# Attention scores in units of three PSUM banks, and diagonal blocks cut at 64, in a layer-norm, attention and expert kernel

## Time and profile before

| what | value |
|---|---|
| median of three runs | 719.63 us (718.04 to 719.94) |
| profiled execution: span from first to last instruction | 717.2 us |
| around the span, by the median | 2.4 us |
| PE busy (matmuls) | 657.9 us, 92% |
| DVE busy | 533.2 us, 74% |
| ACT busy | 497.1 us, 69% |
| POOL busy | 452.1 us, 63% |
| mean granted PE clock | 0.968 |

### The profile page before, as it was taken

One profiled execution on the slowest core, in us unless ns is written; L12 is line 12 of the kernel. 1 busy time (PEld: TensorE's weight loads), 2 busy tenths in 40 slices (PEclk: granted clock), 3 DMA queues, 4 the chain that ended last, 5 costly groups with the idle time before them and its releaser, 6 DMA issues. The chain is left out here.

```text
span 717.2 us, 18299 instructions
## 1 busy us (share of the span) xinstructions
PE 657.9 (92%) x5817; PEld 401.3 (56%) x5817; DVE 533.2 (74%) x1344; ACT 497.1 (69%) x817; POOL 452.1 (63%) x548
## 2 busy tenths in 40 slices
PE   3877468999999999999999999999989999999987
PEld 2765212333333336899999999999943333333323
DVE  7799987888888886554544446666656999999956
ACT  3999357999998996344444444444468899988983
POOL 6465428688888887775600036777636877677782
PEclk9999759999999999999999999999989999999987
DMA  6996595444454447955332234454424544446331
GB/s 172 285 274 216 157 246 102 97 104 86 103 114 103 113 88 186 214 143 144 109 87 73 73 91 120 112 124 114 121 50 80 115 84 109 110 115 128 76 96 37
DMA packets 185863, 89.21 MB, mean 124 GB/s; under 512 B 114608, under 2 KB 175312, under 8 KB 185680
## 3 DMA queue, kind: packets, MB, share of 16 engines
q1 hardware_dynamic: 177472, 70.70, 41.0%
q0 software_dynamic: 8336, 17.84, 9.4%
HBM read 30.17 MB, written 32.24 MB: 87 GB/s over the span
## 5 line engine op out<-in xcount | busy, mean ns | idle before, releaser
L775 ACT ACTIVATE prob<-psum 128x1024 f32<-128x1024 f32 x320 | 314.6, 1026 | 55.3 <-PE psum L867 45.7
L785 ACT ACTIVATE prob<-psum,prob 128x256 f32<-128x256 f32 x284 | 117.3, 470 | 132.3 <-PE psum L997 129.4
L892 PE MATMUL psum<-prob,v 128*18 128x384 f32 (+2 forms) x2560 | 181.3, 392 | 2.2 <-POOL prob L611 1.9
L598 POOL DMA_INDIRECT rows<-slot_y,idx x128 | 132.4, 1034 | 44.0 <-issue 24.0
L600 POOL DMA_INDIRECT slot_x<-rows,slots x128 | 130.1, 1016 | 35.5 <-issue 25.6
L867 PE MATMUL psum<-qks 32*128 32x512 f16 (+3 forms) x1024 | 127.1, 308 | 17.4 <-DMA qks<-dup 9.9
L1013 PEld LDWEIGHTS psum<-prob 128*128 128x128 f32 x1136 | 137.8, 192 | 3.6
L1013 PE MATMUL psum<-prob 128*128 128x128 f32 x1136 | 138.1, 275 | 0.0
L997 PE MATMUL psum<-xs,prob 128*128 128x256 f32 x568 | 134.5, 380 | 1.0 <-DVE xs L1391 0.8
L867 PEld LDWEIGHTS psum<-qks 32*128 32x128 f16 x1024 | 33.9, 93 | 180.1 <-ACT prob L775 91.2
L611 POOL TENSOR_SCALAR_AFFINE_SELECT prob<-prob 128x512 f32<-128x512 f32 x128 | 91.2, 713 | 64.5 <-ACT prob L775 51.4
(11 more groups left out here) (146 smaller groups left out, 640.6 us busy)
## 6 DMA issues: line engine op xcount, KB each, us to landing
slot_y<-xs SPq DMA_DIRECT2D x71, 128.0 KB
xs<-in_L_attn_x SPq DMA_DIRECT2D x16, 256.0 KB, 4.1
prob<-in_L_ffn_W SPq DMA_DIRECT2D x16, 256.0 KB, 3.6
xn_rows<-prob SPq DMA_DIRECT2D x16, 256.0 KB, 2.7
xn_cols<-xts SPq DMA_DIRECT2D x16, 256.0 KB, 3.0
xt<-xn_cols SPq DMA_DIRECT2D x16, 256.0 KB
rows<-xn_rows SPq DMA_DIRECT2D x16, 256.0 KB, 3.1
out<-acc SPq DMA_DIRECT2D x15, 256.0 KB, 2.6
```

The source lines that it names most:

```text
L598: pool.indirect_dma_start(rows[:, j, c, t, :], None, done, where).then_inc(moved[j], 16)
L775: act.activation(prob[:, q % 2, KEPT[u], :], score[(q + u) % 2], ACT.Exp, scale=SCALE / UP ** 2).then_inc(exp_done, 1)
L785: act.activation(hs[:, s, c, :], psum[:, 2 * s + c // 2, (c % 2) * FT:(c % 2 + 1) * FT], ACT.Gelu, bias=ws[:, s, B1C + c:B1C + c + 1]).the ...
L892: mm = pe.matmul(ps_octet[w // 2][32 * g:32 * g + VW, first:first + cols], lhs, prob[:, w % 2, KEPT[u], c:c + cols], start=(i == 0 and not ...
```

## The change

- A score unit becomes three banks, 1536 columns; a batch has 12 units and 12 exponentials. The pieces of a unit belong to three heads, each on its own 32 rows of the array (`PIECES`, `scores`). `prob` becomes seven buffers of 1536 columns instead of ten of 1024.
- Of a diagonal block (128 keys by 128 queries) the half with late keys and early queries isn't computed. Queries 64 to 127 of the block go with all 128 keys, in the full pieces; queries 0 to 63 go with keys 0 to 63 alone, and two heads share those 128 partitions: one head's 64 keys on partitions 0 to 63, another's on 64 to 127. These triangle pieces (`p0` to `p3`) stand in units 0 and 1 of a batch, 32 matmuls of 64 columns in each. For the second head, the tokens of a tile must stand with their halves exchanged: the projection loads a tile shifted by 64 tokens for a part of its columns (`xt`, `project` with two matmuls), and the order of the weights' columns, of the norms and of the output weights' rows changes with it.
- `weigh` becomes ten chunks: for each half of the heads, four of 512 columns and one for the triangles (`p`, 256 columns), whose values come from a new tile `vp` that DVE fills (`share_values`) and POOL clears once.
- POOL masks the 128 diagonal columns of each full piece, 17 instructions a batch; DVE masks the two triangle units, 1024 columns each (`mask_both`).
- `prepare` becomes `unload` (scale q and k, copy v) and `halve`: the high halves are written once, the low halves once, and two fp16 copies double them.
- PSUM: banks 0 to 5 scores, 6 the output of both halves of the heads, 7 the projections and the output projection. So `weigh` of a half waits until DVE has transposed the half before, and a projection until the one before it is unloaded.
- Order in a batch, PE: units 0 to 11 with, behind unit 0 the chunks 7 and 8 of the batch before, behind 1 a projection, 2 chunk 9, 3 a projection, 4 chunk 0, 5 a projection, 6 chunk 1, 7 a projection, 8 chunk 2, 9 chunks 3 and 4, 10 the output projection, 11 chunks 5 and 6. DVE: scale, tile 0, division of the second half of the batch before, tile 1, the two masks, tile 2, tile 3, `share_values`, division of the first half, `add_attention`; in the second part two `combine` ahead of each tile 0, 2, 3 and behind `share_values`.

The core of the diff follows: of the functions that take another's place the new lines stand here, the old ones in the kernel above.

```diff
-    UN = 5
-    UW = 1024
+    UN, UW = 12, 3 * N
+    KEPT = [0, 1, 2, 3, 4, 5, 6, 2, 3, 4, 5, 6]
+    TILE_AT = (0, 3, 1, 2)
-    PARTS = [(0, 0, P, P, N - P), (0, 0, 0, 0, P), (1, 1, P, P, N - P), (3, 1, 0, 3 * P, P), (2, 4, 0, 2 * P, 2 * P)]
-    KEPT = [0, 2, 1, 3, 4]
+    FULL = {1: [(0, HP, HP, N - HP), (3, 0, N - HP, HP)], 2: [(1, P + HP, P + HP, N - P - HP), (2, 0, 2 * P + HP, P + HP)]}
+    MASK_AT = {1: 0, 2: P}
+    PIECES = ["p0 p1 0A10", "p2 p3 0A11", "0A12 0A13 0A20", "0A21 0A22 0A23", "0B10 0B11 0B12", "0B13 0B20 0B21",
+              "0B22 0B23 1A12", "1A13 1A10 1A11", "1A21 1A22 1A23", "1A20 1B10 1B11", "1B12 1B13 1B20", "1B21 1B22 1B23"]
+    WHERE = {piece: (u, j) for u, unit in enumerate(PIECES) for j, piece in enumerate(unit.split())}
+    CHUNKS = ["0A1", "0A2", "0B1", "0B2", "0p", "1p", "1A1", "1A2", "1B1", "1B2"]
...
+        flat_psum = psum[:].rearrange("p a n -> p (a n)")
+        score = [psum[:, 3 * s:3 * s + 3, :].rearrange("p a b -> p (a b)") for s in range(2)]
+        ps_o, ps_out, ps_pc = psum[:, 6, :], psum[:, 7, :], psum[:, 7, :]
+        ps_pick = psum[:, 7, 0:FFN_TILES]
...
+                cols = batch_cols(b).rearrange("d (t c) -> d t c", t=TB)
+                sp.dma_start(xt[:, :, 0:P], cols).then_inc(xt_in, 16)
+                sp.dma_start(xt[:, :, P:P + HP], cols[:, :, 0:HP]).then_inc(xt_in, 16)
...
+            def mask(b, k):
+                for i, (kind, first, n) in enumerate(MASKS[k]):
...
+                    exps_done(UN * b + k + 1)
+                    spot = MASK_AT[int(kind[2])]
+                    parts, base = (P, HP) if kind[1] == "A" else (HP, 0)
+                    p = prob[0:parts, KEPT[k], first * N:(first + n) * N]
+                    p = p.rearrange("p (r c) -> p r c", r=n)[:, :, spot:spot + P]
+                    pool.affine_select(out=p, in_=p, compare_op=ALU.is_ge, fill=0.0, base=base,
+                                       pattern=[[0, n], [0, 2], [1, HP]], channel_multiplier=-1).then_inc(masked, 1)
...
+                for k in range(UN):
+                    act.wait_ge(scored, UN * b + k + 1)
+                    sharing = [u for u in range(UN) if KEPT[u] == KEPT[k]]
+                    if sharing[0] < k:
+                        act.wait_ge(weighed, CN * b + LAST_USE[sharing[0]] + 1)
+                    elif not known(b, 0):
+                        act.wait_ge(weighed, CN * (b - 1) + LAST_USE[sharing[-1]] + 1)
+                    act.activation(prob[:, KEPT[k], :], score[k % 2], ACT.Exp, scale=SCALE / UP ** 2)\
+                        .then_inc(exp_done, 1)
...
+            def project(b, i):
+                t = tile_of(b, i)
+                if i == 0:
+                    pe.wait_ge(xt_in, 32 * (b + 1))
                 if not known(b, 0):
+                    if i == 0 and known(b, 1):
+                        pe.wait_ge(routed, 1)
+                    if i == 0 and some(b - 2):
                         pe.wait_ge(added, b - 2)
+                    pe.wait_ge(proj_evac, TB * b + i)
+                bank = psum[:, t, :] if known(b, 0) else psum[:, 7, :]
+                pe.matmul(bank[:, NAT:NAT + KB], xt[:, t, 0:P], wall[:, 0:KB], start=True, stop=True)
+                pe.matmul(bank[:, NAT + KB:], xt[:, t, HP:HP + P], wall[:, KB:WEND], start=True, stop=True)\
+                    .then_inc(proj_done, 1)
...
+            def queries(ap, kt, first, cols):
+                ap = ap[:, first:first + cols]
+                return ap.rearrange("p (a c) -> p a c", c=HP)[:, ::-1, :] if kt == 2 else ap
+            def scores(b, par, k):
+                n = UN * b + k
+                if k == 0:
                     for t in range(TB):
                         pe.wait_ge(qk_turned[t], 16 * (b + 1))
+                if some(n - 1):
+                    pe.wait_ge(exp_done, n - 1)
+                s = score[k % 2]
+                names = PIECES[k].split()
+                for c in range(2 * TB if names[0][0] == "p" else 0):
+                    o, kt = c // TB, c % TB
+                    for side in range(2):
+                        for j in range(2):
+                            g = 32 * (int(names[j][1]) ^ 2 * side)
+                            low = slice(kt * P, kt * P + HP)
+                            keys = slice(kt * P + HP * side, kt * P + HP * (side + 1))
+                            pe.matmul(s[HP * side:HP * (side + 1), j * N + c * HP:j * N + (c + 1) * HP],
+                                      qks[g:g + 32, par, 1, o + 2 * side, keys],
+                                      qks[g:g + 32, par, 0, 2 * o + side, low], start=True, stop=True)
+                full = [(j, name) for j, name in enumerate(names) if name[0] != "p"]
+                for i in range(2):
+                    for j, name in sorted(full, key=lambda x: -int(x[1][2])):
+                        kt, col, first, cols = FULL[int(name[2])][i]
+                        g, slab = 32 * row_group(name), 2 * int(name[0]) + (name[1] == "B")
+                        keys = qks[g:g + 32, par, 1, int(name[0]) + 2 * (name[1] == "B"), kt * P:(kt + 1) * P]
+                        mm = pe.matmul(s[:, j * N + col:j * N + col + cols], keys,
+                                       queries(qks[g:g + 32, par, 0, slab], kt, first, cols), start=True, stop=True)
+                mm.then_inc(scored, 1)
...
+            def weigh(b, par, c):
+                chunk = CHUNKS[c]
+                o = int(chunk[0])
+                if c == 0:
+                    pe.wait_ge(proj_evac, TB * (b + 1))
+                    if known(b, 0):
+                        pe.wait_ge(routed, 1)
+                if c in (0, 5) and some(2 * b + o):
+                    pe.wait_ge(o_evac, 2 * b + o)
+                if chunk[1] == "p":
+                    pe.wait_ge(masked2, 2 * b + 2)
+                    pe.wait_ge(vp_ready, b + 1)
+                    for kt in range(TB):
+                        for g in range(QH):
+                            u, j = WHERE[f"p{g}"]
+                            col = j * N + (TB * o + kt) * HP
+                            mm = pe.matmul(ps_o[32 * g:32 * g + VW, kt * P:kt * P + HP],
+                                           vp[:, par, kt * H // 2 + QH * o + g, :], prob[:, KEPT[u], col:col + HP],
+                                           start=(c == 5 and kt == 0), stop=(c == 4 and kt == TB - 1),
+                                           skip_group_check=True)
                 else:
+                    pe.wait_ge(masked, MN * b + MASKED[max(units_of(chunk))])
+                    for i in range(2):
+                        kt, col, first, cols = FULL[int(chunk[2])][i]
+                        for g in range(QH):
+                            u, j = WHERE[f"{chunk}{g}"]
+                            odd = (DH + 1) * (chunk[1] == "B")
+                            mm = pe.matmul(queries(ps_o[32 * g:32 * g + VW], kt, first, cols),
+                                           pairs[par][:, kt * H // 2 + QH * o + g, odd:odd + VW],
+                                           prob[:, KEPT[u], j * N + col:j * N + col + cols],
+                                           start=(c == 0 and i == 0), stop=(c == CN - 1 and i == 1),
+                                           skip_group_check=True)
+                mm.then_inc(weighed, 1)
...
+                for k in range(UN):
+                    scores(b, par, k)
+                    if k == 0 and not fresh:
+                        weigh(b - 1, 1 - par, 7)
+                        weigh(b - 1, 1 - par, 8)
+                    elif k == 2 and not fresh:
+                        weigh(b - 1, 1 - par, 9)
+                    elif k in (1, 3, 5, 7) and not last and not known(b, 0):
+                        project(b + 1, k // 2)
+                    elif k in (3, 5, 7) and known(b, 0):
+                        project(b + 1, k // 2 - 1)
+                    elif k in (4, 6, 8):
+                        weigh(b, par, k // 2 - 2)
+                    elif k == 9:
+                        weigh(b, par, 3)
+                        weigh(b, par, 4)
...
+                    elif k == 10 and not known(b, 0):
...
+                        out_project(b - 1, TB * (b + 1) if last else TB * (b + 2))
+                    elif k == 11:
+                        weigh(b, par, 5)
+                        weigh(b, par, 6)
+                    if known(b, 0) and k == 8:
                         project(b + 1, 3)
...
+            def unload(b, par, i):
+                tile, t = TB * b + i, tile_of(b, i)
+                if i == 0:
                     dve.wait_ge(rn_done, 2 * b + 2)
                 dve.wait_ge(proj_done, tile + 1)
                 if some(tile):
+                    dve.wait_ge(lo_done, tile)
+                bank = psum[:, t, :] if known(b, 0) else psum[:, 7, :]
...
+                dve.tensor_tensor(qn[:], bank[:, NAT + HP + E:NAT + VB].rearrange("p (h d) -> p h d", d=DH), scale, ALU.mult)\
+                    .then_inc(qn_done, 1)
```

(65 more changed lines are left out.)

377 lines of the change are left out of this document (129 added, 248 removed).

## The result

The changed kernel takes 737.98 us (median of 4 executions, 736.47 to 740.22) against 719.79 (718.04 to 720.09): ratio 1.026, 95% interval [1.024, 1.029], slower. 714.0 was forecast: the time lies inside the forecast's range, but the kernel became slower where it was to become a little faster. Medians here are over all executions and ratios over undisturbed ones alone; the two differ visibly only for the run that moves the gathers.

What follows compares the result with a forecast made beforehand. PE was taken as the limit in batches 2 to 7, PE and VectorE in 9 to 14; -3.0, -1.5, +3.9, -3.8 and -1.2 total -5.6, so 719.6 becomes 714.0 us, range 690 to 742.

Steps and rivals of the forecast that it cites:

- the cover of the transposes: SP's queue, end of each batch: last tile ready some 4 us before the next batch's first score, landing 3.2 after issue.
- a rival at 0.18: Attention batches: the clock falls, 3.4 us a batch at half rate, 15 x 1.7 = +25, total 739; chance 0.18.
- a hole of 2 us: PE ahead of the fourth projection: waits some 2 us in each batch for VectorE to unload tile 2.
- The circle: PE and VectorE waiting for each other through shared output and projection banks: 21.1 us a first-part batch, 22.65 a second-part one.
- the ends: Last batch and tail: last batch 20.8 instead of 24.56 us, -3.8, and tail -1.2.
- PE work: PE in each batch: units, chunks and projections sum to 18.2 us, some 2.9 less than before.
- Triangle unit: Two units a batch on PE, 32 matmuls of 64 columns and one full piece each: 0.8 us.
- Tile: VectorE preparing a tile: 1.75 us undisturbed, taken as 2.0, bounds 1.6 and 2.5.
- Masks: VectorE in each batch: two masks of 1024 columns replace four of 512, 2.3 us instead of 2.5.
- Exponential: ScalarE: 12 exponentials of 1536 columns a batch, 1.40 us each, 16.8 instead of 20.5; brings nothing by itself.
- the rival of 0.17: Triangle units on PE: small matmuls don't overlap, 1.5 us each in single file, +22, total 736; chance 0.17.
- The tail: After the last exponential: one chunk of 0.99 us left instead of three groups, -1.2 of 8.85.

Runs made afterwards that it cites:

- the run that moves the gathers: On the reordered kernel with late additions and early loads, second-part gathers moved behind units 0 and 5 to 11: 719.52 us, ratio 0.995.
- The order on SP alone: Changed kernel with the last tile's transpose issued ahead of the two loads of x in SP's queue: 723.80 us, ratio 1.003.
- the filled kernel: Changed kernel with transposes ahead of loads, plus two matmuls with unused results in PE's hole ahead of the fourth projection: 714.74 us, ratio 0.995.
- reordered kernel: Transposes-ahead-of-loads kernel with tile 0 projected early, tile 1 ahead of the division, tile 2 unloaded before masks: 722.84 us; with late additions and early loads, 717.45.

## Why the prediction was wrong, point by point

- **The step that failed first** is the cover of the transposes: the new load, put ahead of a transpose "which waits for VectorE anyway some 2 us longer" and costed at nothing, and the landing, "covered, barely". Between batches 3 and 4 tile 3 was ready 0.24 us after SP began with the loads, not some 2 us later. The transpose went out 1.2 us late, PE waited 5.75 us from its issue instead of the 3.2 allowed for, and the hole was 2.51. The order on SP alone is worth 14 us (738.0 to 723.8), 16.5 by the ratios. The forecast had said that each us later would be a us of the batch, and then priced none.
- **The step that failed second** is the choice to hold the clock at 1.00 in the forecast and put its fall into a rival at 0.18. The forecast itself put a hole of 2 us into every batch. Filling the hole against the fall is worth 6 to 9 us with the transposes on time (by ratios and by times). The rival's 739 lies near the 738 measured, but that is luck: its mechanism alone is 6 to 9 us of the 25 that it added, and three of the six falls in the first part stood behind holes at the head of a batch, which the forecast had as covered.
- **The circle held.** With both faults mended (the filled kernel) batches 2 to 7 took 125.6 and batches 9 to 14 took 135.9; the forecast's 6 x 21.1 and 6 x 22.65 are 126.6 and 135.9. The total, 714.7, is the forecast's 714.0. That agreement is partly luck: the ends below missed, the kernel carries matmuls that the forecast doesn't have, one batch of the second part took 24.95 at clock 0.86, and the same second part took 140.98 in another run.
- **Sizes.** PE work: 18.1 a batch at full clock (108.75 over six, reordered kernel), forecast 18.2. Triangle unit: 0.69 from start to start (186.97 to 187.66), and 0.77 where the clock was still low (191.06 to 191.83), forecast 0.8. Tile: 1.6 and 2.2 in batch 11 (612.34 to 613.98, 616.33 to 618.57), around the forecast's 2.0. Masks: 2.4, forecast 2.3. Exponential: 1.45, forecast 1.40.
- **The small matmuls overlap.** 32 of them take 0.38 between starts (186.97 to 187.35), where a unit of 512 columns takes 0.32, so the rival of 0.17 is out. The Trainium skill, TensorEngine Tiling (Array Packing), Restrictions and Gotchas, says that different row tiles cannot access one PSUM bank at once. By the forecast's reading of it a unit would be near 1.0; the trace shows no such price where two row groups write the two partition halves of a bank.
- **The ends.** The last batch took 23.40 (forecast 20.8): PE waited 4.31 us there for a mask behind gathers (row below). The forecast had kept 4 us in which ScalarE is idle; it was idle 6.65 of the 23.40, and behind the wait PE ran at 0.50 again (711.89 to 715.00). The tail took 8.76 instead of 7.65. Start and expert part together cost 2.0 that the forecast did not have. These sum to some 5.7 us of the 23.1 between forecast and measured span; the first part gives 12.4, the second 5.4, batches 0, 1 and 8 give 0.5 back.
- **Open.** Why GpSimd is late in batch 12. PE waits 2.99 us for a mask there in the changed kernel, and as long with SP's order and with the fill. Moving the gathers took that wait from 3.96 to 2.40 us in the reordered kernel, not away. Also open is why some holes of over 2 us had no fall of the clock behind them.
- **GpSimd in the last batch.** The kernel puts all eight gathers of this batch behind its first four units, two behind each. Four of them, of 0.94 to 1.74 us, ran between 705.33 and 711.02, ahead of the mask that PE waited for. The wait in the last batch of the changed kernel, from the timeline of PE:

```profile
711.89 1.91 PE L968 MATMUL psum<-prob,v 128*18 128x448 f32 x16 [4.31 <-POOL prob L680]
```

## What to carry to other kernels

When an engine stops being the limit, ask what its new holes do to its clock before counting the time gained; here 1.6 us of useless work in one hole of each batch gave back 6 to 9 us in all. A DMA "covered, barely" is a term of the sum: work out when its source is ready, what stands ahead of it in its queue, and price the hole and what follows it. Don't count on opening a circle between two engines by moving one step inside it: in the second part the hole moved to a later place, and with several steps moved the next queue (loads, gathers, masks) closed the circle.

## What the runs showed of the hardware

- Holes of 2.51 and 2.66 us were followed by 3.4 and 6.8 us at half rate, although PE had been busy 17.6 of the 22.1 us before the first. The length of the hole alone doesn't tell: a hole of 1.46 us was followed by a fall in the changed kernel (249.15), and holes of 2.67 and 2.28 us by none with the transposes ahead of the loads. In the reordered first part PE's longest hole in batches 5 and 6 was 0.78 us, and all six batches ran at 1.00.
- The transpose issued behind two loads on the same queue was waited for 5.75 us after its issue; in the whole kernel before, the median to landing was 3.2.
